# The residual image of the last stage on 128 partitions, even rows below and odd rows above

## The reference, cut to what matters

```python
# layer 0, its end
y = (y - mu) * lax.rsqrt(var + 1e-05) * ln_g + ln_b
y = y * jax.nn.silu(z)
x = x + jnp.einsum('bhwd,cd->bhwc', y, out_proj_w)
# layer 1
xu = _upsample_rfft(transpose(_gn(x)))
h = transpose(xu) @ W1.T + b1
h = coef[:, 0] + coef[:, 1] * h + coef[:, 2] * (h * h)
h = h @ W2.T + b2
x = x + _lpf_rfft(transpose(h), cutoff=0.5)[:, :, ::2, ::2]
```

## Time and profile before

| | |
|---|---|
| median of 3 runs | 11577.95 us (11575.34 to 11589.02) |
| the profiled execution | 11574.58 us |
| its span, first to last instruction | 11572.8 us |
| PE busy over the span | 84% |
| DVE, ACT, POOL busy over the span | 87%, 74%, 79% |
| PE in the last six of 40 slices | 9 tenths or more |

### The profile page before, as it was taken

The page is one execution under the profiler, slowest core; times in us unless marked ns, Lnnn a source line. Parts: engine busy times, 40 slices in busy tenths (PEclk is TensorE's granted clock), DMA queues, the critical chain, the costliest instruction groups (busy, mean ns, idle before and its releaser), DMA issues. The chain is left out here.

```text
span 11572.8 us, 332532 instructions
## 1 busy us (share of the span) xinstructions
PE 9678.0 (84%) x136268; PEld 6104.2 (53%) x136268; DVE 10116.4 (87%) x6303; ACT 8511.6 (74%) x15618; POOL 9157.8 (79%) x3978
## 2 busy tenths in 40 slices
PE   8967888788888788888787778888888887999999
PEld 5644444444444444444444444444444444788778
DVE  7879999999999999999999999999999996555554
ACT  3468888887888788878888888788888884444443
POOL 1169999998999899989999999899999996433330
PEclk9989999999999999999999999999999998999999
DMA  3366676676667766776677666666766674212210
GB/s 103 106 164 169 171 175 171 167 178 168 172 166 174 177 167 164 173 174 168 171 175 178 172 167 171 175 168 171 178 174 166 171 175 111 65 48 67 61 50 12
DMA packets 561649, 1716.32 MB, mean 148 GB/s; under 512 B 147138, under 2 KB 147938, under 8 KB 558344
## 3 DMA queue, kind: packets, MB, share of 16 engines
q1 hardware_dynamic: 560136, 1695.05, 58.4%
HBM read 1319.08 MB, written 375.39 MB: 146 GB/s over the span
## 5 line engine op out<-in xcount | busy, mean ns | idle before, releaser
L975 POOL TENSOR_TENSOR HC<-H,crep 128x1024 f32<-128x1024 f32 x3072 | 7201.2, 2376 | 583.8 <-PE psum L723 416.0
L797 DVE TENSOR_TENSOR_SCAN H<-E,car,psum 128x1024 f32<-128x1024 f32 x2112 | 4868.7, 2336 | 237.4 <-PE psum L701 113.3
L701 PE MATMUL psum<-diag,dluT 128*32 128x128 f32 x98304 | 3350.7, 288 | 1083.0 <-DVE H L797 1049.2
L701 PEld LDWEIGHTS psum<-diag,dluT 128*32 128x32 f32 x98304 | 2852.9, 116 | 2080.8 <-DVE H L797 1887.9
L882 ACT ACTIVATE E<-dlr,am 128x1024 f32<-128x1024 f32 x2816 | 3194.4, 1143 | 1001.7 <-DMA dlr<-scr_dl 519.4
L866 ACT ACTIVATE diag<-idn,blt 128x128 f32<-128x128 f32 x8192 | 2521.6, 389 | 119.8 <-PE psum L701 119.8
L723 PE MATMUL psum<-HC,sely 128*32 128x512 f32 x12288 | 2232.0, 620 | 32.6 <-POOL HC L975 30.9
L775 DVE TENSOR_TENSOR psum<-dur,psum 128x1024 f32<-128x1024 f32 x1280 | 1548.7, 1210 | 114.6 <-PE psum L664 90.4
L797 DVE TENSOR_TENSOR_SCAN H<-E,psum 128x1024 f32<-128x1024 f32 x704 | 1582.1, 2276 | 75.6 <-PE psum L701 45.9
L664 PE MATMUL psum<-sx,selb 96*128 96x512 f32 x2560 | 981.4, 465 | 532.4 <-DVE H L797 522.3
L664 PEld LDWEIGHTS psum<-sx,selb 96*128 96x128 f32 x2560 | 395.4, 190 | 1423.5 <-DVE H L797 1139.3
(11 more groups left out here) (143 smaller groups left out, 9796.9 us busy)
## 6 DMA issues: line engine op xcount, KB each, us to landing
dur<-scr_dlu SPq DMA_DIRECT2D x3072, 128.0 KB, 4.0
dlr<-scr_dl SPq DMA_DIRECT2D x3072, 128.0 KB, 3.8
crep<-scr_bc SPq DMA_DIRECT2D x1024, 256.0 KB, 5.2
scr_dlu<-dlu SPq DMA_DIRECT2D x256, 384.0 KB, 4.6
scr_yk<-yt SPq DMA_DIRECT2D x256, 384.0 KB, 3.0
brep<-scr_bc SPq DMA_DIRECT2D x512, 128.0 KB, 3.5
scr_dl<-dlt SPq DMA_DIRECT2D x128, 384.0 KB, 5.6
scr_dl<-yt SPq DMA_DIRECT2D x128, 384.0 KB, 3.3
```

The costliest lines, as they stand in the source:

```text
L701: r = e.matmul(P[un % 2][32 * q:32 * q + 32, i * 128:(i + 1) * 128], dluT[:, m % 2, i, 32 * j:32 * j + 32], diag[:, i, at + q, :], start=T ...
L797: e.tensor_tensor_scan(H[:, un % NH, ::step], decay[:, ::step], drive[:, ::step], init, ALU.mult, ALU.add).then_inc(scan_done)
L975: e.tensor_tensor(HC[:, un % NHC, :], H[:, un % NH, :], crep[:, GREP.index(g), :], ALU.mult).then_inc(hc_done)
```

## The change

In `x1` a picture now lies on all 128 partitions: the pixels of its even rows on partitions 0 to 63, those of its odd rows on 64 to 127, one partition for each column as before, and in the free dimension 96 channels x 32 rows. Two pictures stand side by side in the free dimension, `[128, 2, 96, 32]`. The host lays out the input `xh` and the result to match, and a further constant `upH` (tile `uth`) holds the resampling matrix with its even rows first, for `wide`. Eight picture rows, not four, go into one job of the projection, so the gather has 28 jobs for each picture and not 36. The numbers in the diff are those of one file and the other.

```diff
-    x1 = T("x1", [128, C, HW])
+    HH = HW // 2
+    x1 = T("x1", [128, 2, C, HH])
...
-              (w2s[:], "w2T"), (co[:], "coef"), (b2[:], "b2"), (ut[0:64, :], "upT"), (ut[64:128, :], "upT"),
+              (w2s[:], "w2T"), (co[:], "coef"), (b2[:], "b2"), (ut[0:64, :], "upT"), (ut[64:128, :], "upT"), (uth[:], "upH"),
...
                 if t >= FIRST:
-                    yield ("project", b, 2 * (t - FIRST)), side_ve
-                    yield ("project", b, 2 * (t - FIRST) + 1), side_ve
+                    yield ("project", b, t - FIRST), side_ve
...
     def xb(b):
-        lo, hi = half(b)
-        return x1[lo:hi, :, :]
+        return x1[:, b % 2, :, :]
...
                 if t >= FIRST:
-                    for n in (2 * (t - FIRST), 2 * (t - FIRST) + 1):
-                        o = take(e, ("project", b, n))
-                        e.wait_ge(gated, 8 * b + n // 2 + 1)
-                        for w in range(4):
-                            for h in range(2):
-                                r = e.matmul(o[lo:hi, w * C:(w + 1) * C], yv[:, h, 4 * n + w, :], wo[:, h, :], start=h == 0,
-                                             stop=h == 1)
-                        r.then_inc(projected)
+                    n = t - FIRST
+                    o = take(e, ("project", b, n))
+                    e.wait_ge(gated, 8 * b + n + 1)
+                    for w in range(4):
+                        for h in range(2):
+                            for at in (0, 64):
+                                r = e.matmul(o[at:at + 64, w * C:(w + 1) * C], yv[:, h, 8 * n + 2 * w + at // 64, :], wo[:, h, :],
+                                             start=h == 0, stop=h == 1)
+                    r.then_inc(projected)
...
             for i in range(4):
                 for at, c in ((0, 0), (64, HC2)):
-                    r = e.matmul(o[at:at + 64, i * NU:(i + 1) * NU], xb(b)[:, 4 * n + i + c, :], ut[lo:hi, :], start=True, stop=True)
+                    for w in (0, 64):
+                        p = at + w // 2
+                        r = e.matmul(o[p:p + HH, i * NU:(i + 1) * NU], xb(b)[w:w + 64, 4 * n + i + c, :], ut[w:w + 64, :],
+                                     start=True, stop=True)
...
-            e.matmul(o[lo:hi, :], dn[:], t2[:, 8 * n:8 * n + 8, 0:HW], start=True, stop=True).then_inc(down_h_done)
+            for at in (0, 64):
+                r = e.matmul(o[at:at + 64, 0:8 * HH], dn[:], t2[:, 8 * n:8 * n + 8, at // 64:HW:2], start=True, stop=True)
+            r.then_inc(down_h_done)
...
-                    for n in (2 * (t - FIRST), 2 * (t - FIRST) + 1):
-                        v = xb(b)[:, :, 4 * n:4 * n + 4]
...
-                        e.tensor_tensor(v, v, bank(("project", b, n))[lo:hi, 0:4 * C].rearrange("p (w c) -> p c w", c=C),
-                                        ALU.add).then_inc(side_ve)
+                    n = t - FIRST
+                    v = xb(b)[:, :, 4 * n:4 * n + 4]
...
+                    e.tensor_tensor(v, v, bank(("project", b, n))[:, 0:4 * C].rearrange("p (w c) -> p c w", c=C),
+                                    ALU.add).then_inc(side_ve)
...
-                e.tensor_reduce(s12[lo:hi, 0, at:at + HC2], xb(b)[:, c0:c0 + HC2, :], AX.X,
+                e.tensor_reduce(s12[:, 0, at:at + HC2], xb(b)[:, c0:c0 + HC2, :], AX.X,
                                 ALU.add).then_inc(reduced)
```

More of the change, by code:

```diff
@@ L1015, in post_phase @@
     ut = T("ut", [128, NU])
+    uth = T("uth", [128, NU])
     dn = T("dn", [NU, 64])
@@ L1172, in wait_added @@
             e.wait_ge(added, adds(b, n))
-    def half(b):
-        return 64 * (b % 2), 64 * (b % 2) + 64
     def xb(b):
-        lo, hi = half(b)
-        return x1[lo:hi, :, :]
-    def xsq(b):
-        lo, hi = half(b)
-        return y[lo:hi, :, :].rearrange("p a l -> p (a l)")[:, 0:HW * C].rearrange("p (c w) -> p c w", w=HW)
+        return x1[:, b % 2, :, :]
+    xsq = y[:].rearrange("p a l -> p (a l)")[:, 0:C * HH].rearrange("p (c h) -> p c h", h=HH)
     SLOTS = IDLE + NT + NLN + 6 + 4
@@ L1310, in gather @@
             for i in range(2):
-                r = e.matmul(o[:, i:i + 1], s12[lo:hi, i, :], one[lo:hi, 0:1], start=True, stop=True)
+                r = e.matmul(o[:, i:i + 1], s12[:, i, :], one[:, 0:1], start=True, stop=True)
             r.then_inc(stat1)
@@ L1326, in up @@
         def up(b, n):
-            lo, hi = half(b)
             o = take(e, ("up", b, n))
             if n == 0:
-                e.wait_ge(side_ve, count(("project", b, 15)))
+                e.wait_ge(side_ve, count(("project", b, 7)))
             if b:
@@ L1359, in wide @@
                 for at in (0, 64):
-                    r = e.matmul(o[at:at + 64, i * NU:(i + 1) * NU], t1v[at:at + 64, :, COLS * t + i], ut[at:at + 64, :],
+                    r = e.matmul(o[at:at + 64, i * NU:(i + 1) * NU], t1v[at:at + 64, :, COLS * t + i], uth[at:at + 64, :],
                                  start=True, stop=True)
@@ L1441, in gather @@
                 if t >= FIRST:
-                    for n in (2 * (t - FIRST), 2 * (t - FIRST) + 1):
-                        v = xb(b)[:, :, 4 * n:4 * n + 4]
-                        if n == 0:
-                            e.wait_ge(x1_in[b % 2], 16 * (b // 2 + 1))
-                        e.wait_ge(projected, 16 * b + n + 1)
-                        e.tensor_tensor(v, v, bank(("project", b, n))[lo:hi, 0:4 * C].rearrange("p (w c) -> p c w", c=C),
-                                        ALU.add).then_inc(side_ve)
+                    n = t - FIRST
+                    v = xb(b)[:, :, 4 * n:4 * n + 4]
+                    if n == 0:
+                        e.wait_ge(x1_in[b % 2], 16 * (b // 2 + 1))
+                    e.wait_ge(projected, 8 * b + n + 1)
+                    e.tensor_tensor(v, v, bank(("project", b, n))[:, 0:4 * C].rearrange("p (w c) -> p c w", c=C),
+                                    ALU.add).then_inc(side_ve)
                 yield
             yield
-            e.wait_ge(side_ve, count(("project", b, 15)))
+            e.wait_ge(side_ve, count(("project", b, 7)))
             e.wait_ge(pool_set, 2)
@@ L1460, in gather @@
             for c0, at in ((0, 0), (HC2, 64)):
-                e.tensor_reduce(s12[lo:hi, 1, at:at + HC2], xsq(b)[:, c0:c0 + HC2, :], AX.X,
+                e.tensor_reduce(s12[:, 1, at:at + HC2], xsq[:, c0:c0 + HC2, :], AX.X,
                                 ALU.add).then_inc(reduced)
@@ L1498, in down_h @@
             e.wait_ge(down_h_done, 12 * b + n + 1)
-            e.tensor_tensor(xc, xc, bank(("down_h", b, n))[lo:hi, :].rearrange("p (c w) -> p c w", w=HW), ALU.add).then_inc(main_ve)
+            e.tensor_tensor(xc, xc, bank(("down_h", b, n))[:, 0:8 * HH].rearrange("p (c h) -> p c h", h=HH), ALU.add).then_inc(main_ve)
         def wide(b, t):
@@ L1568, in gather @@
                 yield
-            e.wait_ge(side_ve, count(("project", b, 15)))
-            e.wait_ge(projected, 16 * (b + 1))
+            e.wait_ge(side_ve, count(("project", b, 7)))
+            e.wait_ge(projected, 8 * (b + 1))
             for i in range(4):
-                e.activation(xsq(b)[:, 24 * i:24 * i + 24, :], xb(b)[:, 24 * i:24 * i + 24, :], ACT.Square).then_inc(x_squared)
+                e.activation(xsq[:, 24 * i:24 * i + 24, :], xb(b)[:, 24 * i:24 * i + 24, :], ACT.Square).then_inc(x_squared)
                 yield
@@ L1712, in resample @@
                     v = xb(b)[:, 24 * i:24 * i + 24, :]
-                    e.tensor_tensor(v, v, crb[lo:hi, 24 * i:24 * i + 24].unsqueeze(2).to_broadcast([64, 24, HW]),
+                    e.tensor_tensor(v, v, crb[:, 24 * i:24 * i + 24].unsqueeze(2).to_broadcast([128, 24, HH]),
                                     ALU.add).then_inc(bias_added)
@@ L1776, in constants @@
             "upT": np.ascontiguousarray(up.T).astype(f),
+            "upH": np.ascontiguousarray(np.tile(np.concatenate([up.T[0::2], up.T[1::2]]), (2, 1))).astype(f),
             "dnT": np.ascontiguousarray(dn.T).astype(f)}
@@ L1800, in lay_out @@
         "xT": x.reshape(NB, L, C).transpose(0, 2, 1),
-        "xh": x.transpose(0, 2, 3, 1).reshape(NB, HW, C * HW),
+        "xh": x.reshape(NB, HW // 2, 2, HW, C).transpose(0, 2, 3, 4, 1).reshape(NB, 128, C * HW // 2),
         "winT": wi.T,
@@ L1833 @@
         S[name] = nc.dram_tensor(f"in_{name}", a.shape, mybir.dt.from_np(a.dtype), kind="ExternalInput").ap()
-    S["out"] = nc.dram_tensor("out_0_dram", (NB, HW, C * HW), F32, kind="ExternalOutput").ap()
+    S["out"] = nc.dram_tensor("out_0_dram", (NB, 128, C * HW // 2), F32, kind="ExternalOutput").ap()
     build_program(nc, S)
     r = _run(nc, [arrays], core_ids=[0])
-    return np.asarray(r.results[0]["out_0_dram"]).reshape(NB, HW, C, HW).transpose(0, 3, 1, 2)
+    return np.asarray(r.results[0]["out_0_dram"]).reshape(NB, 2, HW, C, HW // 2).transpose(0, 4, 1, 2, 3).reshape(NB, HW, HW, C)
```

## The result

The changed kernel takes 11387.76 us in the median (11369.34 to 11405.1, 4 runs), the kernel before 11576.65 beside it (4 runs): a ratio of 0.9834, 95% interval 0.982 to 0.9849, a gain of 174 to 208 us. The forecast was 11408, a gain of 169. The profiled execution took 11369.34 with a span of 11367.5, 205 less than that of before, more than the medians differ. So I read the last stage alone, from SP's first issue of a constant to the end of the span: 9691.8 to 11572.8 before, 1881.0 us; 9663.9 to 11367.5 after, 1703.6: 177.4 less. The other 28 lie in the scan, which the change doesn't touch.

What follows compares the result with a forecast made beforehand. PE was taken to bound the last stage, so time leaving its list leaves the total. Terms 73.9 + 40 + 41.3 + 17 - 3.4 - 0.5 + 1 = 169.3 took 11574.6 to 11405.3, median 11408; range 11375 to 11495.

Steps and rivals of the forecast that it cites:

- projection pairs, pictures 1 to 7: Projection slots on PE: matmuls alternating between column halves overlap in pairs, 1.32 us less a slot, 73.9 us in all.
- the wait and the clock behind it: Projection slots t = 7 and 8: PE's wait for ACT's variance read goes, 5.7 us a picture, 40; bounds 28 and 43.
- `down_h`: Edge: one matmul of 512 columns becomes two overlapping ones of 256, 0.43 us less a job, 41.3 us.
- picture 0 up to its statistics: Picture 0: shorter slots, no wait at t = 7 and halved DVE reductions gain 17 us; one more constant costs 0.5.
- `up`: Eight matmuls become sixteen on 32 columns each; groups of four overlap, 0.87 us a step, costing 3.4 us.
- last store: End of the stage: 128 rows of half the length land between 0 and 2 us sooner, taken as 1.
- Rival (d): Projection: its pairs don't overlap, only the banks and `down_h` gain; 11493 us, chance 0.06.
- Rival (e): Slots: the wait returns for ACT's round or the variance, the whole 40 us come back; 11448 us, chance 0.07.
- Rival (a): `down_h`: reading every other float costs double; 11449 us, chance 0.12.
- (b): `up`: a group of four costs 124 ns; 11434 us, chance 0.10.
- (c): `up`: matmuls overlap only in pairs; 11529 us, chance 0.05.
- (f): `up`: different row tiles writing one PSUM bank run one by one, making the kernel slower; 11603 us, chance 0.05.

Runs made afterwards that it cites:

- e1: Changed kernel with each projection job doing its eight matmuls into columns 0 to 63 first, then the eight into 64 to 127: 11465.61 us, ratio 0.9904.
- e2: Changed kernel with PE again waiting, midway through the projections t = 7 and 8, for ACT's read of the variance: 11448.69 us, ratio 0.9891.
- e5: Changed kernel with the doubled steps moved to n = 28 and 29 from picture 1 on: 11370.16 us, ratio 0.9812.
- e8: Changed kernel with `down_h` reading 32 floats in a row instead of every other one, so its output is wrong: 11375.58 us, one run.
- e3: Changed kernel with `t1` laid out source pixel first, so the weights of `wide` lie side by side: 11348.74 us, ratio 0.9808.
- e6: Changed kernel with four more filling matmuls between picture 0's statistics matmuls: 11399.3 us, one run; last stage 1703.5, unchanged.
- e7: Changed kernel without the two filling matmuls of each edge step n = 1 to 11: 11356.54 us, ratio 0.9803.

## Why the prediction was right, point by point

The 177.4 us of the last stage can be laid out in time: 16.5 up to picture 0's statistics, 13.7 to picture 1's, 133.7 in the six periods behind (22.3 each), 13.5 from the last statistics to the end. By the steps of the prediction:

| step | forecast | measured |
|---|---|---|
| projection pairs, pictures 1 to 7 | 73.9 | 73 |
| the wait and the clock behind it | 40 | 48 |
| `down_h` | 41.3 | 35.3 |
| picture 0 up to its statistics | 17 - 0.5 | 16.5 |
| `up` | -3.4 | 0 |
| last store | 1 | 4.3 |
| sum | 169.3 | 177 |

- **Projection pairs: right.** PE's time on the line fell by 16.1 a picture, of which 8 x (2.78 - 1.47) = 10.5 are the pairs, 73 in seven pictures. e1 takes them away by order alone: 68.8 with the overlap at the change of halves, (2.51 - 1.47) x 8 x 8 = 66.6 in eight pictures. Rival (d) fell.
- **The wait: right in kind, too small in size.** It went, and none took its place in these slots: a full slot is 9.44 us where 9.5 was forecast, above ACT's 8.80, and the variance doesn't wait from t = 7 on. Rival (e) fell. The remaining 5.6 of the 16.1 and 1.7 that `wide`, the mean, `hidden` and `up` got shorter make 7.3 a picture where 5.7 was taken. 48 is what is left of 177.4 when the other rows are taken off, so it carries their errors; it lies above the stated bounds of 28 and 43. What made it larger is in part argued: the term counted only the stretch behind the wait, but behind the stop of the doubled step `wide` too took longer than its 1.37 us at full clock, 1.71 to 1.88 in the six periods before the change and 1.37 to 1.87 after it. e2, with a wait of 37.3 us in sum, loses 55.3. The prediction also read the timeline as one "with no wait, but for the one in these slots"; the stop of the doubled step, 17.4 us in 8, was there as well, and e5 puts it at 23.4 us.
- **`down_h`: too large by 6 us.** 0.605 instead of 0.57 a job is 96 x 0.035 = 3.4, of which the stride is 2.2 (e8). The rest is the end of the edge: two jobs in a row should have saved 0.86 and saved 0.41, as PE now comes too early for ACT (line 1347 waits for 1602, 1.3 us in 8, as shown above). The step that failed there is "each microsecond that leaves PE's list there leaves the time": the wait for ACT was hidden behind the longer job and isn't behind the shorter one. Rival (a) fell. The rule of the Trainium skill ("Advanced Engine Details and Errata", SBUF cachelines), by which stride 2 is free and stride 100 is not, agrees with the trace but for a few per cent: stride 2 costs 4% of a job (e8), stride 100 costs 124 against 86 ns a pair (e3).
- **`up`: no cost at all.** Groups of four overlap fully, 0.82 us for 32 records, so (b) and (c) fell, and with them the slower one, (f). Neighbours in `up` lie on different rows and write the same bank, and still run together; so do `wide`'s pairs at 86 ns in e3. The rule of the Trainium skill ("TensorEngine Tiling (Array Packing)", Gotcha 1: PSUM Pressure), that different row tiles cannot access one bank at the same time, does not agree with either measurement; here the row tiles write different partitions of the bank.
- **Picture 0: right up to its statistics, to half a microsecond.** The filling is last, as said. The constant was to cost half of 1.22, which is 0.6 and not 0.5; `y`'s first load is issued 0.4 later. Behind the statistics `up` at full clock was left to the low end; it didn't come, and the clock alone would not have helped (e6), as the twelve steps stood behind the load of picture 1. From the statistics to picture 1's, 13.7 are saved where a later period without its `down_h` saves 17.9. From the first statistics matmul to `wide` the changed kernel takes 0.8 more (22.55 for 21.78); the other 3 were not followed.
- **Last store: 4.3 instead of 1.** From its issue to the end of the span it takes 5.5 where it took 9.8, more than the bound of 2 less. That bound had no row of a store from 128 partitions behind it.
- **The whole.** The medians differ by 189, the last stage by 177, which lies within the interval of the medians' difference (174 to 208); the scan's spread is larger than the 12 between them. The sum came closer than its terms: the wait, the last store and `up` brought 8, 3 and 3 more than forecast and `down_h` 6 less. That these cancel in part is luck; that the pairs (e1) and the wait (e2) carry the gain is not.

## What to carry to other kernels

Where TensorE bounds a stage, let neighbouring matmuls alternate between column and row tiles: here a pair or a group of four cost what one did (86 ns for 100 columns), also where its members wrote one PSUM bank on different partitions, and the order of issue alone made 1.47 or 2.51 us of the same 32 records. Count a wait of TensorE with the half clock behind it: here waits of 37.3 us cost 55.3, about 1.5 times their length (e2). Of matmuls that only keep the clock up, try each stretch without them; here real work filled the stretch, and they cost their full length (e7).

## What the runs showed of the hardware that was not expected

- A store of 1.5 MB from 128 partitions landed 5.1 us after its issue, one from 64 partitions with twice the length each 9.3.
- From the start of the 384 records of picture 0's `up` to `wide` it took 18.5 us with picture 1's load beside them and 10.1 us when the load was held back; with the first 220 at full clock (e6) these ran in 5.0 us, and PE then stood longer.
- Weights read 100 floats apart cost `wide` 37% (1.37 against 1.00 us for 20 records); a moving operand read two floats apart cost 4%.
- Matmuls on the other half of the columns start while three records of the half before have yet to start: the change of tile overlaps by 0.27 us.
- The end of the untouched scan lay anywhere between 9660.5 and 9701.7 us in the profiled executions, so stages must be compared from their own start.
